# A GNN and expert layer on one core: whole-block transposes and keep-busy products in the opening, small tables and edge rows asked for later

## The chip, the cores and the metric

The kernel runs on one core of one Trainium2 chip. The metric is the device time of one launch in microseconds (us); the time of a kernel is the median of its runs.

## What is computed

One graph attention layer over 384 nodes of 1024 features, and after it a layer with routed experts. Both start from a layer norm and add to `x`:

```python
def _L0_gnn_ref(x, edge_index, edge_type, edge_type_weights, wq, bq, ...):
    q = x @ wq.T + bq ; k = x @ wk.T + bk ; v = x @ wv.T + bv
    q2 = (q @ wiq.T + biq).reshape(N, H, D).transpose(1, 0, 2)      # k2, v2 alike
    mask = full(-inf); mask[src, dst] = softplus(edge_type_weights)[edge_type - 1]
    scores = einsum('hnd,hmd->hnm', q2, k2) * scale + mask[None]
    out = einsum('hnm,hmd->hnd', softmax(scores), v2)
    return out @ wo.T + bo

x = x + _L0_gnn_ref(_layernorm(x), stack([src, dst]), edge_type_5, ...)
x = x + _L0_ffn_ref(_layernorm(x)[None], ...)[0]                    # attention with routed value and output experts
```

There are 6144 edges. Where an edge occurs more than once, the last one counts.

## The kernel before

**Numbers in two parts.** Every large product is done on a high and a low part: `w_hi` and `hT_hi` are the rounded operands, `w_lo` and `hT_lo` what is left over, and `three` (L1532 to L1534) issues hi·hi, hi·lo and lo·hi. The weights come in *units* of 128x1024 through a ring of three slots: SyncE (SP) loads `w_raw`, ScalarE (ACT) makes `w_hi` (L612, L619), and GpSimd (POOL, L475) or VectorE (DVE, L943) makes `w_lo`, after which SP may load the slot again. A `column_unit` is 24 matmuls of 128x384 and needs the `w_lo` of its unit.

**The opening.** SP asks for `x` (tile 0 in two halves, L359, then tiles 1 and 2, L352), the first weights, and the source and target rows of the first edge piece (L365, L366). ACT asks for four small tables on its own queue: `edge` (L599), `etw`, `bias`, `rs` (L602). Per tile of 128 nodes DVE takes the statistics (L896 to L903), POOL makes `rstd` and `shift` (L467, L470), and ACT normalises tiles 0 and 1 (L624), DVE tile 2 (L935). TensorE (PE) turns each tile by halves of 64x64 (`turn_by_halves`, L1586) into two PSUM banks, ACT writes `hT_hi` (L631) and DVE `hT_lo` (L910), six pieces each. PE waits for all of `hT_lo` before unit 0. On DVE five small instructions on the edge table (L919 to L925) stand between the statistics of tile 0 and of tile 1, and `etw_abs` (L933) right after the statistics.

**The first stage.** Eight turns of three units (q, k, v); unit 3j+i is the i-th of turn j. The turn's `w_lo` for slot 0 comes from POOL, those for slots 1 and 2 from DVE. At its side the mask is built: 6144 edges in eight pieces of six columns. For piece j, ACT asks for its rows (L635, L636, in the turn before it), DVE makes the keys (L957), finds repeats (L965) and makes `cell` (L972), and POOL issues six scatters (L479) into `mask_scratch` in DRAM, and behind them the `w_lo` of unit 3j+6. Before a piece's first scatter POOL waits until all scatters of the piece before have landed. ACT loads the finished mask (L705) behind the `w_hi` of its unit in the second stage, and DVE needs it for the first scores (L1034), which softmax, transposes (L1579) and the second stage's products follow.

**Order.** Every engine's program is written out by hand in its own block; `with ....Fori` is a loop of that engine. An engine does its instructions in this order. What the change touches: ACT L596 to L664, DVE L905 to L946, PE L1589 to L1605, and line L661.

## Time and profile before

| | us |
|---|---|
| runs | 830.97, 829.83, 830.85 |
| median | 830.85 |
| profiled execution | 828.53 |
| its span, first to last instruction | 826.3 |
| TensorE busy in it | 807.2 (98%) |

The profiled execution is one of its own, 2.32 us below the median of the runs; 2.23 us of it lie outside the span. Times in the rows are counted from the span's start. A row of the timeline gives start, duration, engine, line, operation, and in brackets how long the engine had been idle and who ended that; a queue's name with q (ACTq, SPq) is the issue of a DMA, not its transfer.

### The profile page before, as it was taken

The numbers are of one execution on the slowest core, as the hardware profiler recorded it, in microseconds if no ns is written. First come the engines' busy times: TensorE is split into PE (matmuls) and PEld (weight loads), VectorE is DVE, ScalarE is ACT, GpSimd is POOL, SyncE is SP. The second block draws the span as 40 slices with busy tenths as digits, with TensorE's granted clock in tenths as the row PEclk, the third lists the DMA queues.
The fourth block names the chain that finished last, engine by engine and source line by source line (L and its number), as shares of the span: only waits on it lengthen the run. The fifth ranks groups of instructions, "written<-read, shape, count | busy, mean of one in ns | idle before, by whom it ended". The sixth has DMA issues, their size and how long they took to land.

```text
span 826.3 us, 14202 instructions
## 1 busy us (share of the span) xinstructions
PE 807.2 (98%) x5039; PEld 647.0 (78%) x5039; DVE 489.8 (59%) x1108; ACT 376.4 (46%) x614; POOL 462.7 (56%) x297
## 2 busy tenths in 40 slices
PE   3999999999999999999999999999999999999998
PEld 3999998888888789898678578578578588588476
DVE  6988873445444257898644554654655645645545
ACT  5333335655665353334624634634634534525531
POOL 4567776343334435547564664665574665655652
PEclk9999999999999999999999999999999999999999
DMA  7656663442222338533498497497597597697684
GB/s 283 187 177 199 185 208 110 148 131 87 91 76 77 102 118 316 178 128 128 123 232 320 114 252 290 121 268 268 130 262 266 130 263 264 139 254 264 148 209 178
DMA packets 66178, 153.40 MB, mean 186 GB/s; under 512 B 9392, under 2 KB 22320, under 8 KB 66128
## 3 DMA queue, kind: packets, MB, share of 16 engines
q1 hardware_dynamic: 51472, 120.73, 41.2%
q0 software_dynamic: 10944, 24.82, 16.4%
q10 hardware_dynamic: 3712, 7.18, 3.5%
q8 instruction: 31, 0.51, 0.3%
q14 instruction: 19, 0.16, 0.1%
HBM read 122.06 MB, written 37.97 MB: 194 GB/s over the span
## 4 chain that ended last, share of the span: by engine, by line
PE 82%; DMA 5%; issue 4%; POOL 4%; DVE 3%; ACT 1%; POOLq 0%; SPq 0%; DVEq 0%; ACTq 0%
PE bank L1532 21%; PE bank L1534 20%; PE bank L1533 20%; PE bank L1826 12%; DMA mask_scratch<-scratch,cell 4%; POOL mask_scratch L479 4%; PE bank L1586 2%; PE bank L1649 2%; PE bank L1579 2%; PE bank L1621 2%; DMA x<-in_x 1%; DVE scratch L965 1%; DMA mask<-mask_scratch 0%; ACT scratch L624 0%; DVE hT_lo L910 0%
## 5 line engine op out<-in xcount | busy, mean ns | idle before, releaser
L530 POOL TENSOR_TENSOR w_lo<-w_raw,w_hi 128x1024 fp32r<-128x1024 f32 x69 | 170.7, 2475 | 139.4 <-ACT w_hi L777 137.0
L1532 PE MATMUL bank<-w_hi,hT_hi 128*128 128x512 f32 (+1 forms) x504 | 196.2, 389 | 0.3 <-POOL w_lo L475 0.3
L1534 PE MATMUL bank<-w_hi,hT_lo 128*128 128x512 f32 (+1 forms) x504 | 194.0, 385 | 0.0
L1533 PE MATMUL bank<-w_lo,hT_hi 128*128 128x512 f32 (+1 forms) x504 | 193.8, 385 | 0.0
L475 POOL TENSOR_TENSOR w_lo<-w_raw,w_hi 128x1024 fp32r<-128x1024 f32 x39 | 95.2, 2443 | 101.2 <-ACT w_hi L612 80.6
L777 ACT ACTIVATE w_hi<-w_raw 128x1024 fp32r<-128x1024 f32 x86 | 90.9, 1056 | 132.8 <-PE bank L1534 101.1
L1532 PE MATMUL bank<-hT_hi,w_hi 128*128 128x384 f32 x320 | 108.5, 339 | 2.8 <-DVE hT_lo L910 2.8
L1532 PEld LDWEIGHTS bank<-w_hi,hT_hi 128*128 128x128 f32 x504 | 95.1, 189 | 19.5 <-issue 0.6
L1534 PEld LDWEIGHTS bank<-w_hi,hT_lo 128*128 128x128 f32 x504 | 94.7, 188 | 19.1
L1533 PEld LDWEIGHTS bank<-w_lo,hT_hi 128*128 128x128 f32 x504 | 94.8, 188 | 17.7
L1533 PE MATMUL bank<-hT_lo,w_hi 128*128 128x384 f32 x320 | 107.5, 336 | 0.0
L1534 PE MATMUL bank<-hT_hi,w_lo 128*128 128x384 f32 x320 | 107.4, 336 | 0.0
L1826 PE MATMUL bank<-late,gcT 128*32 128x512 f32 (+1 forms) x868 | 100.7, 595 | 0.0
L1826 PEld LDWEIGHTS bank<-late,gcT 128*32 128x32 f32 x868 | 26.6, 109 | 57.3 <-issue 55.2
L479 POOL DMA_INDIRECT mask_scratch<-scratch,cell x48 | 54.2, 1128 | 28.1 <-issue 14.4
L1532 PEld LDWEIGHTS bank<-hT_hi,w_hi 128*128 128x128 f32 x320 | 60.6, 190 | 8.0 <-issue 5.0
L1532 PE MATMUL bank<-large,w_hi 128*128 128x384 f32 x192 | 65.8, 343 | 0.0
L1534 PE MATMUL bank<-large,w_lo 128*128 128x384 f32 x192 | 64.2, 335 | 0.0
L1533 PE MATMUL bank<-large,w_hi 128*128 128x384 f32 x192 | 64.2, 334 | 0.0
L1362 DVE COPY late<-late 128x1024 f32 x56 | 60.2, 1106 | 5.9 <-issue 5.0
L1533 PEld LDWEIGHTS bank<-hT_lo,w_hi 128*128 128x128 f32 x320 | 60.5, 189 | 0.0
L1534 PEld LDWEIGHTS bank<-hT_hi,w_lo 128*128 128x128 f32 x320 | 60.5, 189 | 0.0
(213 smaller groups left out, 1249.0 us busy)
## 6 DMA issues: line engine op xcount, KB each, us to landing
w_raw<-in_units SPq DMA_DIRECT2D x145, 512.0 KB, 4.1
late<-in_units SPq DMA_DIRECT2D x56, 512.0 KB, 7.9
scratch<-slots_scratch SPq DMA_DIRECT2D x7, 512.0 KB, 7.0
scratch<-in_src_row ACTq DMA_DIRECT2D x8, 384.0 KB, 4.2
scratch<-in_dst_row ACTq DMA_DIRECT2D x8, 384.0 KB, 5.6
sums_scratch<-zeros SPq DMA_DIRECT2D x1, 1536.0 KB, 8.1
sums_scratch<-x SPq DMA_DIRECT2D x1, 1536.0 KB, 9.8
x<-sums_scratch SPq DMA_DIRECT2D x3, 512.0 KB, 4.3
```

Source lines behind the costliest of these rows:

```text
L475: pool.tensor_tensor(w_lo[:, s, :], w_raw[:, s, :], w_hi[:, s, :].bitcast(fp32), ALU.subtract).then_inc(lo_ready[s], 1)
L479: pool.indirect_dma_start(out=mask_dram, out_offset=bass.IndirectOffsetOnAxis(ap=cells, axis=0), in_=values, in_offset=None, bounds_check= ...
L530: pool.tensor_tensor(w_lo[:, s, :], w_raw[:, s, :], w_hi[:, s, :].bitcast(fp32), ALU.subtract).then_inc(lo_ready[s], 1)
L777: act.activation(w_hi[:, s, :], w_raw[:, s, :], ACT.Copy).then_inc(hi_ready, 1)
L1362: dve.tensor_copy(copied[:, m % COPY_BUFS, :], late[:, bass.ds(copy_value[m // 2], D)]).then_inc(copied_dve, 1)
L1532: pe.matmul(dst, a_hi, b_hi, start=first, stop=False)
L1533: pe.matmul(dst, a_hi, b_lo, start=False, stop=False)
L1534: return pe.matmul(dst, a_lo, b_hi, start=False, stop=last)
L1579: return pe.transpose(dst, src, ident[:])
L1586: last = pe.transpose(banks[g][:, i * GD:(i + 1) * GD], block[rows, :], ident[rows, rows])
L1621: last = pe.matmul(bank[NT * head + t][:, 0:N], a[p, tok], b[p, :], start=n == 0, stop=n == 2)
L1826: last = pe.matmul(bank[YF[r % 2][f]][lane * LANE:(lane + 1) * LANE, :], gcT[:, r // 4, c:c + LANE], weights, start=True, stop=True)
```

## The change

In the opening, (1) ACT waits for the first half of `x` before it asks for the small tables; (2) `w_hi` of unit 0 is made between the normalising of tiles 0 and 1, not behind both; (3) a tile is turned in eight whole 128x128 transposes, four to a bank, and a bank is handed on after its four; ACT and DVE copy the banks as 4x128 blocks; (4) PE multiplies the identity with itself 14, 6 and 3 times into bank 1, around the transposes; (5) unit 0 is done as eight hi·hi, eight lo·hi and eight hi·lo products, which wait for `hT_hi`, for `w_lo` and for `hT_lo` in that order; (6) ACT makes `w_hi` of unit 2 before the exponential of the table, and DVE does its six small instructions on the tables after `hT_lo` and the `w_lo` of unit 1. In the first stage, (7) ACT asks for the rows of the next piece after its second copy of a turn, not after its first. The transposes of the second layer norm stay as they are (their functions lose an argument).

```diff
@@ scalar
             act.activation(warm[:], minus_half[:], ACT.Exp).then_inc(act_warm, 1)
+            act.wait_ge(x0_landed, 16)
             act.dma_start(edge[:], edge_cols).then_inc(edge_landed, 16)
...
+            def first_hT_his(t):
+                for f in range(2):
+                    act.wait_ge(normed_T, 2 * t + f + 1)
+                    act.activation(whole_to(hT_hi, t, f), whole_from(t, f), ACT.Copy).then_inc(hT_hi_done, 1)
...
             normalise(0, 0)
+            hi_fixed(0, fresh=True)
             normalise(0, 1)
-            hi_fixed(0, fresh=True)
-            hT_his(0, 0)
-            hT_his(0, 1)
-            hT_his(0, 2)
+            for t in range(NT):
+                first_hT_his(t)
             hi_fixed(1, fresh=True)
+            hi_fixed(2, fresh=True)
             act.wait_ge(etw_abs_ready, 1)
             act.activation(w8[:], etw_abs[:], ACT.Exp, scale=-1.0).then_inc(etw_exp, 1)
-            hi_fixed(2, fresh=True)
...
-                    if i == 0:
+                    if i == 1:
                         act.wait_ge(keys_made, j + 1)
                         load_rows(j + 1)
@@ tensor
+            def keep_warm(times):
+                for _ in range(times):
+                    pe.matmul(bank[1][:, 0:P], ident[:], ident[:], start=True, stop=True)
+            def first_normed_turns(t):
...
+                for f in range(2):
+                    for k in range(4):
+                        last = turn(bank[FIRST_BANKS[2 * t + f]][:, k * P:(k + 1) * P],
+                                    normed[:, t, (4 * f + k) * P:(4 * f + k + 1) * P])
+                    last.then_inc(normed_T, 1)
...
-            for t in range(NT):
-                normed_turns(0, t)
-            pe.wait_ge(hT_lo_done, LN_STEPS)
-            for i in range(3):
+            keep_warm(14)
+            first_normed_turns(0)
+            keep_warm(6)
+            first_normed_turns(1)
+            first_normed_turns(2)
+            keep_warm(3)
+            pe.wait_ge(hi_ready, 1)
+            pe.wait_ge(hT_hi_done, LN_STEPS)
+            for k in range(KT):
+                pe.matmul(bank[0][:, 0:N], w_hi[:, 0, k * P:(k + 1) * P], hT_hi[:, k, :], start=k == 0, stop=False)
+            unit_ready(0, 0)
...
+            for i in range(1, 3):
                 column_unit(0, i, bank[i], hT_hi, hT_lo)
```

On VectorE the change is one of order. From the end of the statistics to the first keys it stands before as follows (`etw`, `edge`, `key`, `code`, `kind`, `w` are small tables, `scratch<-x,moments,rstd` is the normalising of tile 2):

```order
SCALAR_TENSOR_TENSOR etw_abs<-etw 128x4
TENSOR_SCALAR scratch<-x,moments,rstd 128x1024
TENSOR_TENSOR hT_lo<-bank,hT_hi 128x8x64 x6
TENSOR_TENSOR w_lo<-w_raw,w_hi 128x1024
TENSOR_SCALAR w<-w 128x4
SCALAR_TENSOR_TENSOR scratch<-scratch 128x768
```

And with the change, the same place on VectorE:

```order
TENSOR_SCALAR scratch<-x,moments,rstd 128x1024
TENSOR_TENSOR hT_lo<-bank,hT_hi 128x4x128 x6
TENSOR_TENSOR w_lo<-w_raw,w_hi 128x1024
SCALAR_TENSOR_TENSOR etw_abs<-etw 128x4
CAST key<-edge 128x48
TENSOR_SCALAR code<-edge 128x48
SCALAR_TENSOR_TENSOR key<-edge,key 128x48
TENSOR_SCALAR code<-code 128x48
CAST kind<-code 128x48
TENSOR_SCALAR w<-w 128x4
SCALAR_TENSOR_TENSOR scratch<-scratch 128x768
```

Six small instructions have moved from ahead of the normalising of tile 2 to just ahead of the keys of piece 0.

On ScalarE, from the normalising of tile 0 to the DMAs of the diagonal, before:

```order
ACTIVATE scratch<-x,shift,rstd 128x1024 x2
ACTIVATE w_hi<-w_raw 128x1024
ACTIVATE hT_hi<-bank 128x8x64 x6
ACTIVATE w_hi<-w_raw 128x1024
ACTIVATE w<-etw_abs 128x4
ACTIVATE w_hi<-w_raw 128x1024
ACT_TABLE_LOAD
```

And with the change:

```order
ACTIVATE scratch<-x,shift,rstd 128x1024
ACTIVATE w_hi<-w_raw 128x1024
ACTIVATE scratch<-x,shift,rstd 128x1024
ACTIVATE hT_hi<-bank 128x4x128 x6
ACTIVATE w_hi<-w_raw 128x1024 x2
ACTIVATE w<-etw_abs 128x4
ACT_TABLE_LOAD
```

The first `w_hi` stands one place earlier, and the exponential has both later `w_hi` ahead of it and only the table load behind it.

## Rows read from the trace of the kernel before

**Rows 1.** The page's part 1: busy us, share of the span, instructions.
```profile
PE 807.2 (98%) x5039; PEld 647.0 (78%) x5039; DVE 489.8 (59%) x1108; ACT 376.4 (46%) x614; POOL 462.7 (56%) x297
```

**Rows 2.** Timeline of PE: the opening, and the one later wait.
```profile
8.57 1.12 PE L1586 MATMUL bank<-ident,scratch 64*128 64x64 f32 x16 [8.57 <-ACT scratch L624]
...
16.96 0.69 PE L1532 MATMUL bank<-hT_hi,w_hi 128*128 128x384 f32 x1 [2.77 <-DVE hT_lo L910]
...
19.99 0.34 PE L1532 MATMUL bank<-hT_hi,w_hi 128*128 128x384 f32 x1
...
39.26 0.33 PE L1532 MATMUL bank<-hT_hi,w_hi 128*128 128x384 f32 x1
...
55.90 0.33 PE L1532 MATMUL bank<-hT_hi,w_hi 128*128 128x384 f32 x1
...
139.27 0.33 PE L1579 MATMUL bank<-ident,scratch 128*128 128x128 f32 x1 [1.36 <-DVE scratch L1047]
```

**Rows 3.** Busy by stretches: from:to, length, engines, PEclk, DMA share, GB/s.
```profile
4.00:5.50 1.50, 0.00 (x0) 0.00 (x0) 0.84 (x2) 0.00 (x0) 0.00 (x0) 1.00 0.34 47
5.50:10.00 4.50, 1.12 (x16) 0.96 (x16) 3.42 (x15) 1.24 (x1) 1.09 (x3) 1.00 0.99 387
```

**Rows 4.** Timeline of ACT, the opening.
```profile
11.68 1.04 ACT L619 ACTIVATE w_hi<-w_raw 128x1024 fp32r<-128x1024 f32 x1
12.62 3.01 ACT L631 ACTIVATE hT_hi<-bank 128x512 fp32r<-128x512 f32 x6
...
17.63 1.28 ACT L649 ACT_TABLE_LOAD   x1
```

**Rows 5.** Timeline of DVE, opening, first turn and later ones.
```profile
7.81 1.29 DVE L896 BATCH_NORM_STATS2 stats<-x 128x6 f32<-128x512 f32 x2 [0.88 <-DMA x<-in_x]
...
12.21 0.81 DVE L935 TENSOR_SCALAR scratch<-x,moments,rstd 128x1024 f32<-128x1024 f32 x1 [0.86 <-POOL shift L470]
...
17.96 2.34 DVE L948 TENSOR_SCALAR w<-w 128x4 f32<-128x4 f32 x1
21.08 0.15 DVE L983 SCALAR_TENSOR_TENSOR w<-etw,etw_abs 128x4 f32<-128x4 f32 x1
...
35.46 1.22 DVE L943 TENSOR_TENSOR w_lo<-w_raw,w_hi 128x1024 fp32r<-128x1024 f32 x1
...
101.73 0.17 DVE L972 SCALAR_TENSOR_TENSOR cell<-scratch,key  x1
```

**Rows 6.** Timeline of POOL: `shift` of tile 2, `w_lo`, scatters.
```profile
11.98 0.19 POOL L470 TENSOR_TENSOR shift<-neg_mean,rstd 128x1 f32<-128x1 f32 x1
...
17.69 2.58 POOL L475 TENSOR_TENSOR w_lo<-w_raw,w_hi 128x1024 fp32r<-128x1024 f32 x1 [2.44 <-ACT w_hi L619]
...
30.25 1.20 POOL L479 DMA_INDIRECT mask_scratch<-scratch,cell  x1 [2.18 <-DVE scratch L999]
...
52.65 2.44 POOL L475 TENSOR_TENSOR w_lo<-w_raw,w_hi 128x1024 fp32r<-128x1024 f32 x1
```

**Rows 7.** Later timeline rows: whole transposes; rows asked for; last scatter of piece 5.
```profile
157.36 0.71 PE L1579 MATMUL bank<-ident,scratch 128*128 128x128 f32 x5
...
98.20 0.34 ACTq L635 DMA_DIRECT2D scratch<-in_src_row  x1
...
101.60 0.97 POOL L479 DMA_INDIRECT mask_scratch<-scratch,cell  x1 [0.30 <-issue]
```

**Rows 8.** Landing: scatters of 97.17, 98.45, 101.60, 126.41; slot-2 weights of 99.3.
```profile
mask_scratch<-scratch,cell POOLq DMA_INDIRECT x1, 2.3
...
mask_scratch<-scratch,cell POOLq DMA_INDIRECT x1, 6.4
...
mask_scratch<-scratch,cell POOLq DMA_INDIRECT x1, 4.3
...
mask_scratch<-scratch,cell POOLq DMA_INDIRECT x1, 2.1
...
w_raw<-in_units SPq DMA_DIRECT2D x1, 512.0 KB, 6.0
```

More of the change, by code:

```diff
@@ L917, in _, with make_lo @@
             layer_moments(0)
+            for t in range(1, NT):
+                dve.wait_ge(x_landed[t], 16)
+                layer_stats(t, 0)
+                layer_stats(t, 1)
+                layer_moments(t)
+            dve.wait_ge(rstd_ready, NT)
+            dve.tensor_scalar(normed[:, NT - 1, :], x[:, NT - 1, :], moments[:, NT - 1, 0:1], rstd[:, NT - 1:NT],
+                              ALU.subtract, ALU.mult).then_inc(last_normed, 1)
+            for t in range(NT):
+                first_hT_los(t)
+            def make_lo(turn, s):
+                dve.wait_ge(hi_ready, turn * RING + (s + 1))
+                dve.tensor_tensor(w_lo[:, s, :], w_raw[:, s, :], w_hi[:, s, :].bitcast(fp32),
+                                  ALU.subtract).then_inc(lo_ready[s], 1)
+            make_lo(0, 1)
+            dve.wait_ge(consts_landed, 16 * 3)
+            dve.scalar_tensor_tensor(etw_abs[:], etw[:], -1.0, etw[:], ALU.mult, ALU.max).then_inc(etw_abs_ready, 1)
             dve.wait_ge(edge_landed, 16)
@@ L1598, in _ @@
             pe.wait_ge(pool_consts, 2)
-            for t in range(NT):
-                normed_turns(0, t)
-            pe.wait_ge(hT_lo_done, LN_STEPS)
-            for i in range(3):
+            keep_warm(14)
[9 more added lines that the diff above has]
+            unit_ready(0, 0)
+            for k in range(KT):
+                pe.matmul(bank[0][:, 0:N], w_lo[:, 0, k * P:(k + 1) * P], hT_hi[:, k, :], start=False, stop=False)
+            pe.wait_ge(hT_lo_done, LN_STEPS)
+            for k in range(KT):
+                last = pe.matmul(bank[0][:, 0:N], w_hi[:, 0, k * P:(k + 1) * P], hT_lo[:, k, :], start=False,
+                                 stop=k == KT - 1)
+            last.then_inc(unit_used, 1)
+            for i in range(1, 3):
                 column_unit(0, i, bank[i], hT_hi, hT_lo)
```

57 lines of the change are left out of this document (26 added, 31 removed).

## The prediction, before the result was known

> **What bounds the kernel now.** I read the page's busy shares first, then the timeline of each engine over the opening and the first stage, then the landing times of single DMAs. TensorE is busy for 807.2 of 826.3 us [rows 1], so a change that touches only the opening and the side work of the first stage can win little: PE's first stage matmul starts at 16.96 us, which is nearly all of the idle time there is, and behind it there is one visible wait, 1.36 us at 139.27 for the first softmax [rows 2]. From 19.99 on PE runs a matmul every 0.17 us without a gap; the nine before it take 3.03 us together, so the first ones run at half rate (the granted clock reads 1.00 all the while [rows 3], so it is the pitch that shows 1.2 against 2.4 GHz). A unit is 24 matmuls, 4.16 us; a turn is 12.48 us.
>
> Beside PE run two chains that are almost as tight. GpSimd: six scatters (about 7.4 us from first to last issue), then the slot-0 `w_lo`. The one for unit 9 runs from 52.65 to 55.09, and PE starts unit 9 at 55.90 [rows 2, 6]: 0.81 us to spare. The next piece's scatters start only when the last scatter has landed. And VectorE: the `w_lo` of unit 5 is done at 36.68, PE needs it at 39.26 [rows 2, 5]: 2.6 us to spare. **So PE can gain in the first stage only what these chains gain, plus 0.81 us.** An earlier PE alone turns into a wait for `w_lo`.
>
> **Part 1, tables asked for later.** Between 4.00 and 5.50 us the DMA engines are 34% busy at 47 GB/s, behind it 99% at 387 GB/s, while `x` tile 1 is already asked for and DVE waits for it until 7.81 [rows 3, 5]. The only new traffic in the hole is that of the small tables. If they move behind, tile 1 can come earlier by the hole, 1.5x(1-47/387)=1.3 us, and by an estimated 0.4 for the ramps at its edges, 1.7 us; at least 0, if the delay lies in the transfer itself. I take 1.7, since the queue is full behind the hole. The Trainium skill (Perfetto Trace Analysis, DMA Instruction — HWDGE) says that the block that generates descriptors is shared by the issuing sequencers and locked for one at a time, which is what would put the tables' descriptors ahead of tile 1; by it the gain is the whole hole, and this trace agrees as far as the hole goes. Tile 1's and tile 2's statistics and `shift` then move from 11.98+0.19=12.17 to 10.47.
>
> **Part 2, `w_hi` of unit 0 first.** In order on ACT it costs 1.04 [rows 4]. It ends near 9.9 (unit 0 lands 1.7 earlier as well), which is before tile 2's `shift` at 10.47. Before, it ended at 12.72, behind it. So what is next on GpSimd after `shift`, the `w_lo` of unit 0 (2.44 us, as the one at 52.65), is now ready when VectorE's normalising of tile 2 is. Before, VectorE started at 12.21, 0.04 us after `shift`, with GpSimd idle. How such a meeting goes, the trace shows: the 128x4 instruction at 17.96, of some 0.15 us, took 2.34 us and ended with GpSimd's `w_lo` (17.69+2.58=20.27) [rows 5, 6]. If GpSimd is first by its 0.04 us, tile 2 is normalised at 10.47+2.44+0.81=13.7; if VectorE is first, at 11.3. I take the first (GpSimd needs no signal from another engine, VectorE does): 0.7 us later than the old 13.02 instead of 1.7 earlier. The Trainium skill (SBUF — State Buffer, § on the shared port pair) states the same as a rule: the pair is an exclusive lock and whichever starts first holds it for its whole instruction. It speaks against this edit.
>
> **Part 3, whole transposes.** Five of 128x128 take 0.71 us [rows 7], so a tile is about 1.1 us, against 1.12 for the sixteen halves at the cold rate [rows 2]: nothing by itself, but the first bank is handed on after four, 0.55. ACT's copies are 3.01/6=0.50 each [rows 4]. Tile 2's two follow 13.7+0.6, so `hT_hi` is complete at about 15.4 (old: 15.63); with VectorE first, at about 13.8.
>
> **Part 4, identity products and three passes.** They lie in PE's idle time, 14 before the first tile arrives. The trace has no such product; bounds are one 128x128 transpose, 0.13 us, and four of them cold, 1 us, for each: 14 take 1.8 to 14 us. At the upper end they would delay tile 0's transposes from 8.6 to 15.6 and cost 5 us; I take 0.2 to 0.4, the rate of a 384-column product, where they end by 7.2. PE then starts unit 0 at 15.5 instead of 16.96 (1.4 us), and if the clock has risen by then, 9 x 0.15 = 1.3 us more. So PE alone is up to 2.8 us early.
>
> **Part 5, the tables on VectorE.** After `w_lo` of unit 1 come six small instructions and only then the exponential's partner. Before, the exponential was long done and ACT's table load (1.28, at 17.63) lay under the 2.34 us block [rows 4, 5]. Now `etw_abs` (two SBUF operands) is itself what is blocked by GpSimd's `w_lo` of unit 2. From the unblocking: table load 1.28, an estimated 0.7 for exponential, logarithm and their signals, and then L983; about 2.0 us, where the old distance is 21.08-20.27=0.8. That adds 1.2 us, less if the load is hidden. All of piece 0 stands behind it: keys, cells, weights, and the diagonal's DMAs, which ACT issues before its copy of unit 0 and the `w_hi` of unit 3.
>
> **Sum for the edge chain.** -0.25 (`hT_hi` 15.4 for 15.63) +1.2 = 0.9 us later: first scatter 31.2 for 30.25, `w_lo` of unit 5 at 37.6, which PE wants at 39.26-2.8=36.5. PE's lead is cut to 1.7 there, and by unit 9 to whatever piece 1's start allows.
>
> **Part 6, rows one unit later.** In each turn the two row loads (384 KB each) go out 4.16 us later. Scatters feel them: at 97.17, before the rows asked for at 98.20, one lands in 2.3 us; at 98.45, 6.4; at 101.60, 4.3, while without rows, at 126.41, 2.1 [rows 7, 8]. The last scatter of a piece sets the next piece's start. Before, it is issued 3.4 us after the rows and lands 2.2 later than it need. With rows 4.16 later and PE not ahead, it goes out 0.8 before them and lands in 2.3: the chain gains up to 1.4 us a piece (then `w_lo` behind the scatters is next) and stops binding. VectorE gets its rows 0.9 us later than it asks; its cells of 101.73 were there 4 us before the scatter of 101.60 had landed, for which the next ones wait [rows 5, 7], so nothing is lost.
>
> **Forecast.** Unit 9 then starts 0.2 to 1.3 us earlier than 55.90; I take 0.7, and as the mask no longer lands after ACT is ready for it, 0.2 of the wait at 139.27. Together -0.9: 828.53 profiled becomes 827.6, and with the 2.3 us between it and the median, **829.9**. Chance 0.42, own range 829.0 to 831.2. A measurement of this kernel can tell 0.2%, 1.7 us, from no change.
>
> **Rival A, the lock falls the other way** (VectorE normalises tile 2 first, or unit 0 comes too late to matter there). Then `hT_hi` is complete at 13.8, the edge chain is 0.7 early instead of 0.9 late, and unit 9 gains 1.6 us more than above: 2 to 3 in all, time 828.2 (827.3 to 828.9). For it: in the old trace VectorE came first; against: GpSimd had nothing to do then. Chance 0.28.
>
> **Rival B, slower: the rows run into the last scatter.** The 4.16 us were worked out for a PE that is not ahead. PE is ahead now by up to 2, and ends up bound by the `w_lo` behind the scatters: then the rows go out 9.1 us after unit 3j+3 starts, and the last scatter 0.5 to 1.3 us after the rows, just where the trace has the 6.4 us landing. A landing of 5.3 us in place of 4.3 makes a piece 8.1+5.3=13.4 us, over PE's 12.48, and PE pays 0.9 us in each of six or seven turns: 5 to 7 us, time 836 (832 to 838). It decides from a last scatter that is issued later than about the rows themselves, and it feeds itself, since each late piece holds PE at the same phase. For it: the phases as computed; against: only the row loads are in flight then, where before the slot-2 weights were too (asked for at 99.3, landed 6.0 later [rows 8]), and if such a landing is under 4.4 us the chain escapes. Chance 0.25.
>
> **Rival C, the hole stays** (the tables' traffic now stands ahead of the first weights, or tile 1 is no earlier). In-order ACT then waits for unit 0 before tile 1, `hT_hi` is complete at 15.9, the edge chain is 1.5 late: 831.3 (830.5 to 832.5). Chance 0.05.
>
> **Numbers.** Range 827.4 to 836.2: it leaves out the best of A and the worst of B. Faster by over 0.2% (under 829.2): all of A and some of the forecast, 0.34. Slower by over 0.2%: most of B, some of C, 0.27. Same: 0.39.
>
> **What would show it.** Tile 1's statistics at 6.1 instead of 7.81 (part 1). The normalising of tile 2 lasting about 3.2 us instead of 0.81 (part 2, against rival A). PE's first matmul near 15.5 and no 0.32 us pitch (part 4). L983 about 2 us behind the unblocking (part 5). Last scatters of the pieces landing in 2.1 to 2.5 us (part 6) or in over 5 (rival B), and with these PE waiting for `w_lo` (L475) at the start of each turn. Wrong altogether would be a PE that loses time behind 140 us, where the change moves nothing.

## The result, and the profile after

The changed kernel takes 833.2 us (median of 8 runs, 831.4 to 835.7) where the kernel before takes 830.4 in the same comparison (8 runs, 828.2 to 831.2): ratio 1.0040, 95% interval 1.0027 to 1.0054. It is slower by 0.4%. The profiled execution took 833.85 us with a span of 832.0, against 828.53 and 826.3 for the one before. Of the page, parts 1 and 4:

```profile
PE 815.5 (98%) x5061; PEld 653.7 (79%) x5061; DVE 493.8 (59%) x1108; ACT 375.9 (45%) x614; POOL 462.6 (56%) x297
...
PE 86%; DVE 4%; DMA 3%; issue 2%; POOL 2%; ACT 1%; another core or an unknown queue 0%; SPq 0%; DVEq 0%; ACTq 0%; POOLq 0%
```

Part 1 answers to [rows 1]: PE is busy 8 us longer. 7.3 of them are the identity products in its idle time at the start (4.93 us in the first row below, 1.50 and 0.83 behind the transposes of tiles 0 and 2). Each of the 23 products in the code shows as two rows, so the x28 of the first row are the 14 of `keep_warm(14)`. By this view the change looks harmless. PE's timeline (columns: start us, length us, engine, line, operation, output<-inputs, count, and in brackets the idle time before it and who ended it):

```profile
1.61 4.93 PE L1611 MATMUL bank<-ident 128*128 128x128 f32 x28 [1.61 <-POOL ident L467]
...
15.96 1.65 PE L1640 MATMUL bank<-hT_hi,w_hi 128*128 128x384 f32 x8 [0.16 <-ACT hT_hi L639]
...
20.22 0.33 PE L1551 MATMUL bank<-hT_hi,w_hi 128*128 128x384 f32 x1
...
70.18 0.44 PE L1551 MATMUL bank<-hT_hi,w_hi 128*128 128x384 f32 x1 [1.36 <-POOL w_lo L483]
...
93.64 0.66 PE L1551 MATMUL bank<-hT_hi,w_hi 128*128 128x384 f32 x1 [2.36 <-DVE w_lo L952]
94.10 0.52 PE L1552 MATMUL bank<-hT_lo,w_hi 128*128 128x384 f32 x1
94.42 0.52 PE L1553 MATMUL bank<-hT_hi,w_lo 128*128 128x384 f32 x1
...
144.99 0.33 PE L1598 MATMUL bank<-ident,scratch 128*128 128x128 f32 x1 [1.35 <-DVE scratch L1066]
```

PE starts unit 0 at 15.96 for 16.96 [rows 2], at full rate from its first matmul (eight in 1.65 us), and unit 1 at 20.22, 2.4 us earlier than before. Then it gives that back: it waits at the start of units 3, 6, 9 and 12 (0.95, 0.38, 0.45 and 1.36 us, all for GpSimd's `w_lo`) and 2.36 us for VectorE's `w_lo` at 93.64, after which nine matmuls in a row start 0.32 us behind the one before instead of 0.17. The first softmax runs at 144.99 for 139.27: 5.7 us late, exactly the difference of the spans. Behind it nothing differs.

What sets that moment is the mask, and so the scatters. GpSimd's timeline, first and last scatters of some pieces and the `w_lo` between them:

```profile
31.93 1.20 POOL L487 DMA_INDIRECT mask_scratch<-scratch,cell  x1 [2.19 <-DVE scratch L1018]
...
39.06 1.28 POOL L487 DMA_INDIRECT mask_scratch<-scratch,cell  x1 [0.30 <-issue]
40.36 2.41 POOL L483 TENSOR_TENSOR w_lo<-w_raw,w_hi 128x1024 fp32r<-128x1024 f32 x1
44.94 1.57 POOL L487 DMA_INDIRECT mask_scratch<-scratch,cell  x1 [2.17 <-DMA mask_scratch<-scratch,cell]
...
90.02 2.38 POOL L483 TENSOR_TENSOR w_lo<-w_raw,w_hi 128x1024 fp32r<-128x1024 f32 x1
96.98 1.36 POOL L487 DMA_INDIRECT mask_scratch<-scratch,cell  x1 [4.58 <-DVE cell L991]
...
111.46 1.36 POOL L487 DMA_INDIRECT mask_scratch<-scratch,cell  x1 [2.86 <-DVE cell L991]
```

The first scatter goes out at 31.93 for 30.25 [rows 6], 1.7 us late. From there to the first scatter of the last piece it is 93.15 us (to 125.08), where it was 88.89 (30.25 to 119.14): 4.3 us more in seven pieces. The mask is asked for at 134.29 for 128.62 (ScalarE's queue, the kernel before and then the changed one):

```profile
128.62 0.40 ACTq L705 DMA_DIRECT2D mask<-mask_scratch  x1
```

```profile
134.29 0.40 ACTq L718 DMA_DIRECT2D mask<-mask_scratch  x1
```

In 18 of the 19 profiles of this document the first softmax starts 10.65 to 10.82 us after this request (w2: 11.29), so it is the mask that places it. **So the ledger is +1.7 in the opening and +4.0 in the turns.** The rows show two different waits: for the landing of the scatters themselves in the early pieces (44.94), and for `cell`, which VectorE makes, in the later ones (96.98, 111.46). Why VectorE is late there:

```profile
86.92 0.96 DVE L976 SCALAR_TENSOR_TENSOR scratch<-scratch 128x768 f32<-128x768 int32 x1 [2.32 <-DMA scratch<-in_dst_row]
...
89.82 3.67 DVE L952 TENSOR_TENSOR w_lo<-w_raw,w_hi 128x1024 fp32r<-128x1024 f32 x1
...
96.04 0.17 DVE L991 SCALAR_TENSOR_TENSOR cell<-scratch,key  x1
```

This is VectorE's timeline. Its keys wait 2.32 us for the rows, and the `w_lo` that follows starts 0.2 us before GpSimd's own of 90.02 and takes 3.67 us where it takes 1.22 alone [rows 5]. PE waits for just that one (93.64). The opening, VectorE's timeline and then GpSimd's:

```profile
6.01 1.29 DVE L909 BATCH_NORM_STATS2 stats<-x 128x6 f32<-128x512 f32 x2 [0.49 <-DMA x<-in_x]
...
11.16 2.82 DVE L944 TENSOR_SCALAR scratch<-x,moments,rstd 128x1024 f32<-128x1024 f32 x1 [0.93 <-POOL shift L478]
...
18.62 2.36 DVE L957 SCALAR_TENSOR_TENSOR etw_abs<-etw 128x4 f32<-128x4 f32 x1
...
22.77 0.16 DVE L1002 SCALAR_TENSOR_TENSOR w<-etw,etw_abs 128x4 f32<-128x4 f32 x1
```

```profile
11.07 2.35 POOL L483 TENSOR_TENSOR w_lo<-w_raw,w_hi 128x1024 fp32r<-128x1024 f32 x1
```

### The profile page after: what moved, and what is told of

It reads as the page before. It is cut to its first block, busy times and chain, and to the rows that moved or that the text cites. A ratio compares the mean times of both kernels' runs of the same rounds, so it can differ in the third digit from the quotient of the medians.

```text
span 832.0 us, 14245 instructions
## 1 busy us (share of the span) xinstructions
PE 815.5 (98%) x5061; PEld 653.7 (79%) x5061; DVE 493.8 (59%) x1108; ACT 375.9 (45%) x614; POOL 462.6 (56%) x297
## 4 chain that ended last, share of the span: by engine, by line
PE 86%; DVE 4%; DMA 3%; issue 2%; POOL 2%; ACT 1%; another core or an unknown queue 0%; SPq 0%; DVEq 0%; ACTq 0%; POOLq 0%
PE bank L1551 23%; PE bank L1553 22%; PE bank L1552 22%; PE bank L1871 12%; PE bank L1605 2%; PE bank L1694 2%; POOL mask_scratch L487 2%; PE bank L1598 2%; PE bank L1666 2%; DMA mask_scratch<-scratch,cell 1%; DMA x<-in_x 1%; DVE scratch L984 1%; DMA scratch<-in_dst_row 1%; DVE w_lo L952 1%
## 5 line engine op out<-in xcount | busy, mean ns | idle before, releaser
L1551 PE MATMUL bank<-hT_hi,w_hi 128*128 128x384 f32 x312 | 106.4, 341 | 5.5 <-POOL w_lo L483 3.1
L1552 PE MATMUL bank<-hT_lo,w_hi 128*128 128x384 f32 x312 | 104.9, 336 | 0.0
L1553 PE MATMUL bank<-hT_hi,w_lo 128*128 128x384 f32 x312 | 104.9, 336 | 0.0
L487 POOL DMA_INDIRECT mask_scratch<-scratch,cell x48 | 54.7, 1139 | 31.6 <-issue 15.5
```

The source lines that it names most:

```text
L487: pool.indirect_dma_start(out=mask_dram, out_offset=bass.IndirectOffsetOnAxis(ap=cells, axis=0), in_=values, in_offset=None, bounds_check= ...
L1551: pe.matmul(dst, a_hi, b_hi, start=first, stop=False)
L1552: pe.matmul(dst, a_hi, b_lo, start=False, stop=False)
L1553: return pe.matmul(dst, a_lo, b_hi, start=False, stop=last)
```

## The experiments

Seventeen kernels, in five comparisons with runs of the kernel before beside them (its medians there: 830.5, 831.1, 830.7, 830.7, 830.5). **All ratios are to the kernel before, with 95% intervals.** Names are those of the expectations. Below, an execution *kept its clock* when its mean granted clock is 0.999 or 1.0, and *lost* it otherwise; the last section shows what that is worth.

| kernel | rows asked in unit | opening | median us | ratio |
|---|---|---|---|---|
| the change | 1 | changed | 833.2 | 1.0040 [1.0027, 1.0054] |
| r1_rows_back | 0 | changed | 829.6 | 0.9990 [0.9978, 1.0001] |
| r2_rows_alone | 1 | before | 834.6 | 1.0045 [1.0031, 1.0059] |
| r3_pool_after_dve | 1 | no lock | 831.6 | 1.0012 [0.9996, 1.0027] |
| r6_both_rows_back | 0 | no lock, tables' work early | 831.1 | 1.0005 [0.9995, 1.0015] |
| u1_more_at_1 | 0, extra 1 | before | 836.9 | 1.0073 [1.0060, 1.0087] |
| u2_more_at_0 | 0, extra 0 | before | 841.4 | 1.0142 [1.0121, 1.0164] |
| t1_lock_rows | 0 | no lock | 828.7 | 0.9966 [0.9952, 0.9979] |
| t2_tables_front | 0 | no lock, tables as before | 828.3 | 0.9966 [0.9953, 0.9978] |
| v1_late_keys | 0, keys held | before | 833.7 | 1.0027 [1.0004, 1.0050] |
| v2_t2_rows_late | 1 | as t2 | 830.6 | 1.0011 [0.9999, 1.0024] |
| t6_front_cold | 0 | as t2, no identity products | 830.5 | 0.9999 [0.9988, 1.0010] |
| t5_hi_late | 0 | no lock, by order | 827.5 | 0.9970 [0.9959, 0.9981] |
| w1_double_at_1 | 1, two buffers | before | 828.3 | 0.9971 [0.9962, 0.9981] |
| w2_double_at_0 | 0, two buffers | before | 831.9 | 1.0015 [1.0003, 1.0028] |
| x1_hi_late_tables_front | 0 | as t5, tables as before | 828.3 | 0.9974 [0.9961, 0.9986] |
| z1_after_double | 1, two buffers | changed | 831.7 | 1.0019 [1.0006, 1.0033] |
| y1_hi_late_double | 1, two buffers | as t5 | 830.0 | 0.9999 [0.9983, 1.0014] |

### The change cut in two

The later rows are one line (ScalarE's loop over pairs). r1 takes it out of the changed kernel, r2 puts it alone into the kernel before:

```diff
-                    if i == 1:
+                    if i == 0:
                         act.wait_ge(keys_made, j + 1)
                         load_rows(j + 1)
```

> The changed kernel with the rows asked for after the first copy of a turn again, as before. Theory R (the row loads run into each piece's last scatter): the last scatters land 2 to 4.5 us after issue, not 5 to 5.3, no piece takes over 12.8 us, PE waits for w_lo at most once after unit 6, and the time is 830.0 (0.4 under the kernel before, 829.0 to 831.0). Theory E (the late start of the edge chain, first scatter at 31.9 instead of 30.25, is the loss): the start is as late as in the changed kernel and so is the time, 832.5 to 833.5.

> The kernel before with only the rows asked for after the second copy of a turn. Theory R says that it depends on the phase: here PE isn't ahead, the last scatter of a piece is issued 0.8 us or more before the rows, lands in 2.1 to 2.5 us from the second piece on, and the time is the kernel before's less up to 0.3 us (829.8 to 831.0). If asking later is bad by itself (VectorE waits for rows, its w_lo meets GpSimd's), it is 832 or more.

Without the later rows the changed kernel is as fast as before (829.6); with them alone the kernel before is as slow as the changed one (834.6). The line costs 0.45 to 0.50% wherever it stands: 1.0040 for 0.9990, 1.0045 for 1, and further down 1.0011 for 0.9966. **The slowdown is the later rows, and it does not need a PE that runs ahead.** It is not the clock either: among the executions that lost it, the change is at 833.2 and r1 at 830.1, r2 at 834.6 and the kernel before beside it at 831.1. VectorE's timeline of r2 shows what my prediction had ruled out:

```profile
34.90 0.96 DVE L957 SCALAR_TENSOR_TENSOR scratch<-scratch 128x768 f32<-128x768 int32 x1 [1.31 <-DMA scratch<-in_dst_row]
...
39.48 2.36 DVE L965 SCALAR_TENSOR_TENSOR scratch<-scratch,key 128x512 bf16<-128x512 f32 x1
...
52.64 3.38 DVE L965 SCALAR_TENSOR_TENSOR scratch<-scratch,key 128x512 bf16<-128x512 f32 x1
...
57.38 0.17 DVE L972 SCALAR_TENSOR_TENSOR cell<-scratch,key  x1
```

The keys of the second piece wait for the rows, 34.90 for 32.54. The repeats behind them, 0.75 us each when free, then meet GpSimd's `w_lo` (2.36 and 3.38 us), and the third piece's `cell` is there at 57.4, not 51.8. The first scatter of that piece goes out at 58.70 instead of 57.30.

### Waiting, or the place of the bytes?

Two theories were left. Theory 1: VectorE's wait costs. Theory 2: 768 KB of rows beside the last scatters of a piece lengthen their landing (the mechanism of rival B). First I tried each apart from the other. u1 and u2 add a second, unread pair of row loads to the kernel before, at the late and at the early place; v1 leaves all rows alone and holds VectorE's keys by a 64-byte transfer:

```diff
+            def load_unread(piece_words, j):
+                unread = y_more[:].bitcast(int32)
+                act.wait_ge(unread_landed, j * 32 + 32)
+                act.dma_start(unread[:, 0, 0:PIECE * P], src_row[piece_words]...)
+                act.dma_start(unread[:, 1, 0:PIECE * P], dst_row[piece_words]...)
...
+                    if i == 1:                      # u1; u2: behind load_rows, i == 0
+                        load_unread(j + 1, j)
...
+                    if i == 2:                      # v1
+                        act.wait_ge(token_landed, j * 16 + 16)
+                        act.dma_start(token[:], src_row[0:1, 0:16]).then_inc(token_landed, 16)
...
                 dve.wait_ge(rows_landed, j * 32 + 32)
+                dve.wait_ge(token_landed, j * 16 + 16)     # v1
```

> The kernel before, with its own rows asked for where they were, in each pair's first unit, and beside them an extra pair of row loads of the same size and source, into a buffer that the first stage does not use, asked for one unit later (and one such pair before the loop). Nothing waits for the extra rows inside the loop. It carries the late traffic of the rows alone, without any late VectorE. Theory 1 (in the kernel before with late rows, 4 us went because VectorE's keys waited for the rows and its repeats then ran into GpSimd's lows): the scatters start as before, 44 to 45 and 57 to 58 us for the second and third piece, and the time is 830 to 831.5. Theory 2 (the row transfer, falling on the last scatters of a piece, makes their landing long and thus the next piece's first scatter late): pieces come at about 13.2 us rather than 12.5 from the fourth on, and the time is 833.5 to 835.

> The same extra pair of row loads in the kernel before, asked for right behind the real ones in the first unit: the same extra bytes, at the place in which the kernel before has its rows. Both theories expect 830 to 831.5, since neither the later wait nor the late traffic is there; if it is as slow as the kernel with the extra rows one unit later, it is the additional bytes that cost and not where they fall.

> The kernel before, rows asked for and landing as in it, but VectorE's key instruction of each later pair also waits for a transfer of 64 bytes that ScalarE's queue asks for in the third unit of the pair before. That transfer should land some 2 us after it is asked, so the keys of the second piece run at about 34.9 us rather than 32.5, as they did with the rows asked for one unit later, while the 786 KB of rows stay where they were. Theory 1 (with late rows the time goes because VectorE is held and its repeats then run into GpSimd's lows): cells at 43 and 57 us for the second and third piece, time 833 to 835. Theory 2 (the rows' bytes beside the last scatters are what costs): the time is 830.5 to 831.5 whatever the cells do.

Neither came out cleanly. The extra bytes cost much more than the bytes' move (836.9), and more at the early place (841.4) than at the late one, against both theories: **the amount of row traffic in a turn has a price of its own, and of the two places the one with both pairs on top of each other was the dearer.** GpSimd's timeline of u2 has the second piece's first scatter at 47.94, for 44.33 before (1.3 us of this its first piece had already, 31.54 for 30.25):

```profile
47.94 1.70 POOL L480 DMA_INDIRECT mask_scratch<-scratch,cell  x1 [5.23 <-DMA mask_scratch<-scratch,cell]
```

v1's twelve executions fall into two groups, four at 827.9 to 828.7 and six at 834.5 to 835.3 (of the other two one took 833.0, and the profiled one 831.8). So holding the keys can cost all that r2 loses, and can cost nothing.

The clean separation keeps the bytes and takes only the wait away. With two row buffers, ScalarE asks for the rows of the piece after the next, so no key ever needs what was just asked for. w1 does it at the late place, w2 at the early one:

```diff
+        both_rows = nc.alloc_sbuf_tensor_at("both_rows", [P, 4 * PIECE * P], ...)   # p (b a n)
...
+            act.wait_ge(rows_landed, 32)
+            load_rows(1, 1)
...
-                    if i == 0:
+                    if i == 1:                      # w2: i == 0
                         act.wait_ge(keys_made, j + 1)
-                        load_rows(j + 1)
+                        act.wait_ge(rows_landed, j * 32 + 64)
+                        load_rows(j + 2, j & 1)
```

> The kernel before with two buffers for the rows: the first piece's as before, the second piece's asked for by ScalarE at some 17 us, and then in each pair the rows of the piece after the next, one unit later than the kernel before asks for its own. Each pair carries the same 786 KB of rows as before, at the later place, but they are wanted only a whole pair later, so that VectorE's keys never wait. Theory 1 (VectorE's wait is the cost of the later rows): the time is that of the same kernel with the rows in the first unit, within 1 us. Theory 2 (the place of the bytes beside the last scatters is the cost): 3 to 4 us more than that kernel, some 834, with the pieces over 13 us apart.

> The same kernel with two buffers, the rows asked for in the pair's first unit, where the kernel before asks for its own. Both theories: 830 to 831.5, that is the time of the kernel before, less or more what the second piece's early rows do to the opening (up to 1 us, since 786 KB more are read at 17 us, beside the weights of the first units).

**The late place is 3.6 us faster than the early one (828.3 for 831.9), once VectorE does not wait.** Half of this is the clock: w1 kept it in all 10 executions (828.3), w2 in 3 of 12 (830.0). The rest still says that in the kernel before theory 2 is wrong in sign, and that what went wrong in r2 begins with VectorE's wait. Against the kernel before itself the late place gains less than the ratio of 0.9971 says: the 18 executions of it that kept the clock are at 828.9, 0.6 us above w1. And w1's profile has no earlier mask (129.63 for 128.62, in an execution whose unit 0 starts 1.2 us late, at 18.12) and in steady state no faster pieces (12.48 us; 12.41 in the kernel before, 12.49 in w2, means of the last four). GpSimd's timelines in steady state, w1 and then r2:

```profile
102.68 0.97 POOL L481 DMA_INDIRECT mask_scratch<-scratch,cell  x1 [0.30 <-issue]
103.67 2.42 POOL L477 TENSOR_TENSOR w_lo<-w_raw,w_hi 128x1024 fp32r<-128x1024 f32 x1
107.73 1.36 POOL L481 DMA_INDIRECT mask_scratch<-scratch,cell  x1 [1.65 <-DVE cell L977]
```

```profile
105.21 0.97 POOL L479 DMA_INDIRECT mask_scratch<-scratch,cell  x1 [0.30 <-issue]
106.19 2.40 POOL L475 TENSOR_TENSOR w_lo<-w_raw,w_hi 128x1024 fp32r<-128x1024 f32 x1
110.76 1.65 POOL L479 DMA_INDIRECT mask_scratch<-scratch,cell  x1 [2.17 <-DMA mask_scratch<-scratch,cell]
```

In w1 the landing is no longer what a piece waits for, but its cells, and pieces come every 12.48 us, PE's own pace. In r2 it is, although its cells are early by then (95.8 for a scatter at 97.57), and pieces come every 13.2 us. The difference is where the rows fall: w1 asks for them 2.1 us after the last scatter (104.75), r2 1.1 us before it (104.10). Over the 17 profiles with the kernel before's amount of rows I took, for each piece whose successor's wait the trace puts down to the landing, the time from the last scatter to the next first one:

| rows asked for, against the last scatter | cases | median us | from, to |
|---|---|---|---|
| 3.0 to 4.8 before | 51 | 5.2 | 4.2, 6.5 |
| 2.0 before | 1 | 6.5 | |
| 0.1 to 1.1 before | 15 | 6.0 | 5.4, 7.1 |
| 1.3 or more after | 0 | | |

In the last row the landing was never the last to come: where `cell` and GpSimd were ready the next piece started 3.6 us after the last scatter. That much of part 6 was right: scatters land sooner when the rows come behind them. **So both theories hold in turn**, as r2's profile has it (v1's two groups say that the first step isn't certain to follow). VectorE's wait pushes two or three pieces back by 1 to 3 us; that puts the last scatters onto the rows; from there the landing alone keeps the pieces at over 12.48 us.

### The same in the changed kernel

> The changed kernel, and its only edit is the second buffer: the second piece's rows are asked for at some 16 us, and in each pair the rows of the piece after the next, in the second unit, where the changed kernel asks for the next one's. If VectorE's wait for the rows is the whole of its loss, the time is at or under that of the changed kernel with the rows back (829.6): 828.5 to 829.5, and no key instruction waits for rows. If the later place of the bytes costs something when PE runs ahead, it is 831 or more.

> The same, and the high part of unit 0's first tile behind ScalarE's two normalisings (no lock on VectorE). If the gains add: the lock's 2.1 (829.6 to 827.5) and the late bytes' 0 to 2, so 826 to 827.5. If the early rows of the second piece spend it in the opening, as PE's first unit was 1.2 us later in the double-buffered kernel before, 828.

z1 is the changed kernel with the two buffers and nothing else, y1 has the lock taken out as well (t5's edit, below). z1 gains on the change (1.0019 for 1.0040) but does not reach r1's 0.9990, and y1 is slower than t5 (0.9999 for 0.9970). Their keys never wait long, yet z1's GpSimd, and its PE, show

```profile
46.04 1.72 POOL L489 DMA_INDIRECT mask_scratch<-scratch,cell  x1 [3.41 <-DMA mask_scratch<-scratch,cell]
```

```profile
57.45 0.44 PE L1556 MATMUL bank<-hT_hi,w_hi 128*128 128x384 f32 x1 [2.01 <-POOL w_lo L485]
```

Here PE is ahead, so the second unit's request comes at 38.78, on top of the last scatter (38.90), and the next piece waits 7.1 us for it; in w1, with PE not ahead, it came 3.9 us after (there the next piece started 6.9 us after the last scatter too, but for its cells). That is rival B, in the place where I had put it, beside VectorE's wait. By the ratios, of the 0.50% (4.1 us) that the later rows cost the changed kernel, VectorE's waits make 0.21% (1.7 us) and the place of the bytes 0.29% (2.4 us); with intervals of some 0.13% to either side, each is good to about 1.5 us. The second figure also holds what the second buffer and its early load cost by themselves, which in the kernel before, at the early place, is 0.15% (w2).

The purest case of rival B is the profile of r3 (described below: the change without the lock), one of that kernel's three slowest executions, 834.2 us with a median of 831.6. No key waits for rows there, yet the rows go out 0.2 to 0.8 us before the last scatter in each of the seven turns, the pieces come every 13.25 us, and PE waits 0.33 to 0.85 us for GpSimd's `w_lo` at seven units. Two of its rows, GpSimd's and then PE's:

```profile
97.11 1.64 POOL L487 DMA_INDIRECT mask_scratch<-scratch,cell  x1 [2.19 <-DMA mask_scratch<-scratch,cell]
```

```profile
94.98 0.44 PE L1552 MATMUL bank<-hT_hi,w_hi 128*128 128x384 f32 x1 [0.45 <-POOL w_lo L483]
```

So in an execution like this one, with PE ahead, VectorE's wait isn't needed for the slowdown, as a PE ahead isn't needed in r2.

v2 is the third context for the late rows, on a mended opening:

> The kernel that has the changed opening with the lock taken out and the tables where they were, and in it the rows of the next piece asked for one unit later again (the one edit of the change that the kernel leaves out). If the late rows cost what they cost in the kernel before (834.6 for 830.5, +4.1) and in the changed one (833.2 for 829.6, +3.6), the time is 828.3 + 3.9 = 832.2, with the scatters of a piece 13.1 to 13.3 us apart. If PE's earlier start had given the rows room, as my prediction had it, it is 828.3 or less.

It lost 0.45% (0.9966 to 1.0011), 3.7 us by the ratios, as expected; the medians, of different comparisons, are only 2.3 us apart. Its keys waited for rows in four of the seven pieces (0.8, 0.7, 1.8 and 0.6 us).

### The opening: lock, tables, identity products

The lock was taken out in two ways, by a wait of GpSimd (r3, t1, t2, v2) and by putting the high part of unit 0's first tile back behind ScalarE's two normalisings (t5, x1, y1):

```diff
             rstds_of(0, 0, NT)
+            pool.wait_ge(last_normed, 1)            # r3, t1, t2, v2, t6
             make_lo(0, 0)
...
             normalise(0, 0)
-            hi_fixed(0, fresh=True)                 # t5, x1, y1
             normalise(0, 1)
+            hi_fixed(0, fresh=True)
```

> The changed kernel, in which GpSimd waits for VectorE's normalising of tile 2 before it makes w_lo of unit 0. The normalising takes 0.8 us instead of 2.8, hT_hi is complete near 14.0 instead of 15.8, the first scatter goes out near 30.1 instead of 31.9. Theory E: the time falls by those 1.8 us, to 831.4. Theory R: by 1.8 too if the collision stays as it is, but PE is again ahead of the scatters by the same phase, so 831 to 832 and no better than the kernel before.

> The changed kernel with both causes taken out: GpSimd's first lows wait until VectorE has normalised tile 2 (no lock on VectorE there), and the rows of the next piece are asked for in the pair's first unit again. If the two are independent, the time is that of the kernel with the rows back (829.6) less what the lock costs, 829.6 - 1.5 = 828.1, with the first scatter at 31.2 and pieces every 12.5 us. If the lock's cost had been hidden behind the scatters' own pace, it is 829.6 again. Over 830.5 would say that the later lows of unit 0 cost PE more than the lock did.

> The changed kernel with the rows back in the first unit, and the high parts of unit 0's first tile made behind ScalarE's two normalisings as in the kernel before, which is what makes GpSimd's lows of unit 0 late. VectorE's normalising of tile 2 should then take 0.8 rather than 2.8 us, without a wait on GpSimd. PE's first matmul waits for that high part instead. 828.7 if the lock is the only thing that it changes (as with the explicit wait of GpSimd), 829.6 if the lock's gain is spent on PE's later start.

VectorE's normalising of tile 2 takes 0.81 us in all of them. r3 against the change: 1.0012 for 1.0040. t1 and t5 against r1: 0.9966 and 0.9970 for 0.9990. **By the ratios the lock costs 0.2 to 0.3%, about 2 us, in either company.** At the same clock it is less: r1 and t5 are at 830.1 and 828.9 among the executions that lost it and at 828.2 (two executions) and 827.0 among those that kept it, 1.2 us apart in both, and r3 is 0.5 us under the change (832.7 for 833.2). t5's rows, VectorE's and then GpSimd's:

```profile
12.18 0.82 DVE L944 TENSOR_SCALAR scratch<-x,moments,rstd 128x1024 f32<-128x1024 f32 x1 [0.93 <-POOL shift L478]
```

```profile
12.77 2.46 POOL L483 TENSOR_TENSOR w_lo<-w_raw,w_hi 128x1024 fp32r<-128x1024 f32 x1 [0.62 <-ACT w_hi L628]
```

The tables: t2 and x1 ask for them at once again and have their instructions where the kernel before has them.

```diff
-            act.wait_ge(x0_landed, 16)
             act.dma_start(edge ...)
```

> The kernel above, and in it the small tables asked for at once (no wait for x tile 0), and the instructions that work on them, with the absolute routing weights and their exponential, where the kernel before has them, ahead of the normalising of tile 2. It keeps of the change the whole transposes, the identity products, the early high parts of unit 0 and the three passes. The edge chain should be as early as before: first scatter at about 30.3 rather than 31.2, so 827 to 828 if the scatters' end sets the stage's end and the PE's early start is not spent by it; equal to the kernel above within 0.5 if the tables' place does not matter.

> The changed kernel with the rows back in the first unit, the high part of unit 0's first tile behind ScalarE's two normalisings (which took the lock away at 827.5), and the small tables, their instructions and the routing weights' exponential where the kernel before has them. It keeps the whole transposes, the identity products and the three passes. If the edge chain's 0.9 us earlier start is worth something to a kernel without the lock: 826.5 to 827. If not, 827.5, as for the one with the explicit wait (828.3 and 828.7 with and without the tables in front).

The first scatter goes out at 30.34 and 30.46 instead of 32.64 (t1) and 31.14 (t5), but the time is the same within what these comparisons tell (0.9966 for 0.9966, 0.9974 for 0.9970). That doesn't make the early start of the edge chain slack. In the profiles of r1, t1, t2, t5, t6 and x1 the mask is asked for 96.9 to 97.0 us after the first scatter, so a later start reaches the softmax in full (x1 138.09, t5 138.82). At the same clock x1 is 0.3 us faster than t5 (826.7 for 827.0 kept, 828.6 for 828.9 lost); the medians hide it, since t5 kept the clock in 7 of 12 executions and x1 in 4. t1's 32.64 comes from an opening of its own (below). r6 moved the tables' instructions forward but asked for the tables late:

> The changed kernel with three edits: GpSimd's wait as in r3; VectorE's small table instructions and the exponential ahead of tile 2's normalising, as soon as the tables are there; rows after the first copy again. The first scatter near 28.6, no piece over 12.8 us. Theory R: 3 to 4 us under the kernel before, 826.5 to 827.5. If the opening's gain can't be carried to the end by anything (another bound in the first stage), 829 to 830.

It did not test what it was made for: VectorE stood 4.6 us waiting for `rs` to land (at 16.6), the first scatter went out at 34.6, and the time (1.0005) says only that this is worse than t1.

Last, the identity products, taken out of t2:

```diff
-            keep_warm(14)
...
-            keep_warm(6)
...
-            keep_warm(3)
```

> The same kernel (lock out, tables where they were, rows asked for in the first unit), without the identity products ahead of the transposes. PE should then make its transposes and the first passes of unit 0 at half the clock: by the 0.32 us pitch of the kernel before for some 8 to 10 matmuls, unit 0 ends about 1.3 us later. If PE's lead is real slack behind the edge chain the time stays at 828.3; if PE sets the end of the stage it is 829.3 to 829.6.

Without them the whole gain is gone: 830.5, 0.9999. PE's timeline of t6, and then of t2:

```profile
13.08 3.29 PE L1598 MATMUL bank<-ident,scratch 128*128 128x128 f32 x16 [2.47 <-ACT scratch L633]
...
17.16 1.62 PE L1637 MATMUL bank<-hT_hi,w_hi 128*128 128x384 f32 x8 [0.80 <-ACT hT_hi L639]
```

```profile
12.83 1.97 PE L1598 MATMUL bank<-ident,scratch 128*128 128x128 f32 x16 [1.84 <-ACT scratch L633]
...
15.84 1.66 PE L1640 MATMUL bank<-hT_hi,w_hi 128*128 128x384 f32 x8 [0.37 <-ACT hT_hi L639]
```

Sixteen transposes take 3.29 us instead of 1.97. It isn't a matter of how often the clock was kept: among the executions that lost it, t6 is at 830.7 and t2 at 828.3. Both kernels run unit 0 at full rate, so the products do not pay through unit 0's pitch, as I had it, but through the transposes: `hT_hi`, VectorE's copies behind it, the keys (21.42 for 20.30) and with them the first scatter (31.48 for 30.34) and the mask (128.48 for 127.26) all come 1.1 to 1.2 us later without them. PE's own start, 1.3 us earlier, is the other difference. The products don't always do it: in t1's profiled execution, the slowest of its five, the sixteen transposes behind them took 3.57 us with the granted clock down to 0.50, which is why its first scatter is as late as 32.64 (PE's timeline, then the busy time of a stretch):

```profile
12.99 3.57 PE L1599 MATMUL bank<-ident,scratch 128*128 128x128 f32 x16 [2.26 <-ACT scratch L634]
```

```profile
14.00:16.00 2.00, 2.00 (x12) 2.00 (x11) 1.84 (x4) 1.45 (x3) 1.68 (x1) 0.50 0.95 315
```

How late the edge chain starts in t1's four other executions isn't known, so its median says nothing about the worth of an early start.

**A version that beats both kernels** is t5, 827.5 us (0.9970), the changed kernel with two lines put back; t1, t2, x1 and w1 are its equals within their intervals.

## Why the prediction was wrong

I forecast 829.9 us (0.42) and gave no change 0.39 and slower 0.27. The time, 833.2, is clearly slower; it lies in the range, in the part that I had given to rival B (832 to 838, 0.25).

- **Part 6 failed, at the step "VectorE gets its rows 0.9 us later than it asks ... so nothing is lost".** The spare time that I read from the cells of 101.73 [rows 5] was there, some 4.6 us at r2's third piece too (in the kernel before its cells are done at 52.0 for a scatter at 57.30, 0.7 of which always pass). The lateness was what I had wrong: I took 0.9 us, for a wait that simply shifts the queue; the keys waited 1.3 and 1.8 us in r2 and up to 2.3 in the change. But in the kernel before VectorE's repeats of that piece fit between two `w_lo` of GpSimd; held by 1.3 to 1.8 us they no longer do, and came out 5.6 us late. And the gain was over-sized: up to 1.4 us a piece was to come from scatters that land sooner, but with VectorE not waiting (w1) pieces keep PE's 12.48 us, and at the same clock that kernel is 0.6 us under the kernel before.
- **Rival B** had the right mechanism for the changed kernel's early pieces (39.06 to 44.94, 52.61 to 59.10: 5.9 and 6.5 us from last scatter to next first). It was over-sized for this kernel (836): I let it run through six or seven turns, which is what r3's profile shows. In the change's profile the collision ends after three. PE waits 1.36 us at 70.18, ScalarE's copy comes late at 80.54, and the rows go out at 80.85, 2.2 us behind the last scatter of 78.61; then VectorE's keys wait (86.92). And its condition, a PE that runs ahead, was not needed for the slowdown, which r2 has as well.
- **Part 1**: the hole did fill. Between 4.00 and 5.50 us the DMA engines move 306 GB/s, where it was 47 [rows 3]:

```profile
4.00:5.50 1.50, 1.50 (x12) 1.50 (x12) 1.35 (x5) 0.00 (x0) 0.00 (x0) 1.00 0.84 306
```

  But tile 1's statistics begin at 6.01 in this profile and at 6.61 in z1's, and at 7.5 to 8.0 in the six other profiles with later tables, as in ten of the eleven with early ones (7.7 to 8.2; 9.0 in w1). The bandwidth of the hole mostly went to other transfers. The rule that I had cited beside it, one descriptor-generating block that is locked for one user at a time (the Trainium skill, Perfetto Trace Analysis, DMA Instruction — HWDGE), may hold; the gain that I had drawn from it came in 2 of 8 profiles.
- **Part 2 was right**: 2.82 us for the normalising of tile 2, blocked by the `w_lo` of 11.07, for an expected 3.2. Rival A did not occur in the profile of the change, nor in r1's. The price, 2 us by the ratios and 1.2 at the same clock, is near that of the rival (829.9 for 828.2). The rule of the Trainium skill (SBUF — State Buffer, SBUF: two separate sides), whichever starts first keeps the pair for its whole instruction, agrees with these rows (GpSimd from 11.07, VectorE from 11.16). By the starts that the trace records it doesn't fit two other rows above: VectorE's 89.82 and r2's 52.64 begin 0.2 and 0.4 us before GpSimd's `w_lo` (90.02, and 53.05 in r2) and still end behind it, so a start a few tenths earlier in the trace doesn't tell who is held.
- **Parts 3 and 4**: PE's first matmul at 15.96 for an expected 15.5, no 0.32 us pitch, the 14 products (x28 in the rows) in 4.93 us, 0.35 each, where I had 0.2 to 0.4. Right in size, but I had written "nothing by itself" for the transposes and counted the clock's gain on PE alone.
- **Part 5 was right**: L1002 starts 1.9 us behind the unblocking (20.90 to 22.77; expected 2.0), and the first scatter at 31.93 for an expected 31.2. How much a late start of the edge chain matters here isn't shown by a pair of its own; t5 against x1, 0.7 us in the first scatter, is 0.3 us in the time at the same clock.
- **The sum without part 6** is worth a look. I had 827.6 profiled, 0.9 us under before, all of it from the rows' move; r1, which lacks the move, measures 829.6, 0.9 under before (0.9990, with an interval up to 1.0001). The agreement is an accident of two errors: by the ratios the opening gains 3 us by the identity products and loses 2 by the lock, and the rows then cost 4.

## What to carry to other kernels

A load that is moved later costs nothing only if its consumer has room at every place, and room is to be read in the consumer's own queue, piece by piece, with the instructions of another engine that can block it there; measured against the end of a distant chain it looks larger than it is. Where a transfer must move, give it a second buffer first, then choose its place: the same line cost 4 us with one buffer, and with two it was the better place by 3.6, half of that by the clock that PE kept. And an edit that lets one engine run ahead changes the phase of every transfer that this engine's progress triggers. Differences of 1 or 2 us are worth reading again among executions of the same clock before they are given to an edit.

## What the runs showed of the hardware that I had not expected

**The same wait sometimes costs the clock.** The kernel before waits 1.36 us at its first softmax [rows 2]. In its profiled execution the granted clock stays at 1.00. In r1's profile the same wait is followed by matmuls 0.32 us apart and a granted clock of 0.50, the 1.2 GHz level, with 1.00 before it (PE's timeline, then the busy time of that stretch):

```profile
140.37 0.33 PE L1598 MATMUL bank<-ident,scratch 128*128 128x128 f32 x1 [1.37 <-DVE scratch L1066]
140.63 1.22 PE L1605 MATMUL bank<-ident,scratch 64*128 64x64 f32 x32
141.78 0.60 PE L1551 MATMUL bank<-large,w_hi 128*128 128x384 f32 x1
142.18 0.52 PE L1552 MATMUL bank<-large,w_hi 128*128 128x384 f32 x1
```

```profile
142.00:144.00 2.00, 2.00 (x7) 2.00 (x7) 0.00 (x0) 2.00 (x5) 2.00 (x13) 0.50 0.17 47
```

Over 129 executions of the kernel before, 18 have a mean granted clock of 0.999 or 1.0 and a median of 828.9 us, the other 111 one of 0.997 or 0.998 and 830.7. So the profiled execution's distance to the median (828.53 for 830.4) is mostly that. The same step shows in the profiles: from that softmax to the end of the span it is 686.8 to 687.1 us in the eleven in which PE keeps its clock there, and 688.4 to 688.6 in six in which it drops (689.8 and 690.2 in w2 and u2), at least 1.3 us for the drop. The variants differ in how often they keep the clock: w1, whose PE waits only 0.58 us there in its profile, in all 10 executions, t5 in 7 of 12, t2 in none of 6. Part of most differences above is this. Where both groups exist, t5 beats the kernel before in either, 827.0 for 828.9 and 828.9 for 830.7.

**One delay stays open.** At 80.54 us of the changed kernel ScalarE's copy waits 4.21 us for a releaser that the trace doesn't name, some 1.6 us more than its usual 2.63, while PE's matmuls show no gap; v2 has a delay of 1.0 us at 79.71, there behind PE's bank. The row request behind it goes out that much later, and the 2.32 us wait of the keys at 86.92 follows from it. I don't know what held it.
